# Attention kernel: shared units in another order, second layer norm on GpSimd, clamp checks in pairs

## What is computed

```python
def xattn(query, key_value, Wq, bq, Wk, bk, Wv, bv, Wo, bo):
    q, k, v = ...
    attn = jnp.einsum('bhqd,bhkd->bhqk', q, k) * scale
    attn = jnp.clip(attn, -CLAMP, CLAMP)
    attn = jax.nn.softmax(attn, axis=-1)
    x = jnp.einsum('bhqk,bhkd->bqhd', attn, v).reshape(B, Nq, Cq)
    return x @ Wo + bo
x = x + jnp.tanh(g_xattn[0]) * xattn(_layernorm(x, axis=-1), ctx_768, ...)
x = x + jnp.tanh(g_ffn[0]) * ffn(_layernorm(x, axis=-1), ...)
```

## Time and profile before

| | |
|---|---|
| median of 3 runs | 2075.0 us (2073.8 to 2075.75) |
| profiled execution | 2074.38 us, of which the span of instructions is 2072.6 us |
| TensorE / VectorE / ScalarE / GpSimd busy | 95% / 61% / 35% / 5% of the span |
| mean granted TensorE clock | 0.975 of full speed |
| attention stage | from about 105 us to 609 us |

### The profile page before, as it was taken

One profiled execution on the slowest core, in us unless ns is written; L12 is line 12 of the kernel. 1 busy time (PEld: TensorE's weight loads), 2 busy tenths in 40 slices (PEclk: granted clock), 3 DMA queues, 4 the chain that ended last, 5 costly groups with the idle time before them and its releaser, 6 DMA issues.

```text
span 2072.6 us, 29677 instructions
## 1 busy us (share of the span) xinstructions
PE 1978.3 (95%) x9252; PEld 1426.3 (69%) x9252; DVE 1271.3 (61%) x2415; ACT 725.1 (35%) x1206; POOL 102.0 (5%) x294
## 2 busy tenths in 40 slices
PE   7899999999958999999999999999999999999998
PEld 5734333333337877888888888888888888888887
DVE  5588888888626675555565465456456546555544
ACT  4447666666722222222222222222222222222222
POOL 4201001110111000000000000000000000000000
PEclk9979999999969999999999999999999999999999
DMA  7832222222110010000010010001010001000100
GB/s 242 328 105 78 78 79 69 80 69 69 38 42 21 0 64 32 31 10 15 26 35 16 31 30 15 10 26 40 11 31 31 15 10 48 18 10 10 46 30 36
DMA packets 76457, 102.47 MB, mean 49 GB/s; under 512 B 29026, under 2 KB 47204, under 8 KB 74340
## 3 DMA queue, kind: packets, MB, share of 16 engines
q1 hardware_dynamic: 76388, 101.67, 15.7%
HBM read 75.81 MB, written 25.56 MB: 49 GB/s over the span
## 4 chain that ended last, share of the span: by engine, by line
PE 69%; DVE 1%; ACT 0%; issue 0%; DVEq 0%; ACTq 0%
PE ps_h L1878 35%; PE ps_y L1892 35%; DVE h_lo L2099 0%; DVE h_hi L2095 0%; ACT gelu L1998 0%; DVE gated L2164 0%; ACT L1998 0%; DVE out_T_acc L2169 0%; DVE w_lo L2040 0%; DVE w_lo L2207 0%; DVE w_hi L2038 0%; PE ps_h L1960 0%; PE ps_h L1928 0%; DVEq L2233 0%; DVEq L2094 0%
## 5 line engine op out<-in xcount | busy, mean ns | idle before, releaser
L1998 ACT ACTIVATE gelu<-ps_h,b 128x512 f32<-128x512 f32 x512 | 352.7, 689 | 1084.1 <-PE ps_h L1878 1018.3
L2095 DVE CAST h_hi<-gelu 128x512 fp32r<-128x512 f32 x512 | 219.7, 429 | 575.6 <-ACT gelu L1998 570.1
L1878 PE MATMUL ps_h<-x_hi,w_hi 128*128 (+1 forms) x1024 | 409.2, 400 | 10.1 <-DVE w_lo L2040 8.8
L1892 PE MATMUL ps_y<-h_hi,w_hi 128*128 128x512 f32 x1024 | 405.1, 396 | 6.1 <-DVE h_lo L2099 6.1
L1878 PE MATMUL ps_h<-x_lo,w_hi 128*128 (+1 forms) x1024 | 406.0, 396 | 0.0
L1878 PE MATMUL ps_h<-x_hi,w_lo 128*128 (+1 forms) x1024 | 405.7, 396 | 0.0
L1892 PE MATMUL ps_y<-h_lo,w_hi 128*128 128x512 f32 x1024 | 404.9, 395 | 0.0
L1892 PE MATMUL ps_y<-h_hi,w_lo 128*128 128x512 f32 x1024 | 404.8, 395 | 0.0
L2099 DVE TENSOR_TENSOR h_lo<-gelu,h_hi 128x512 fp32r<-128x512 f32 x512 | 357.3, 698 | 16.5
L957 DVE TENSOR_REDUCE low<-ps_s 128x1 f32<-128x512 f32 x512 | 321.8, 682 | 41.2 <-PE ps_s L814 39.1
L1071 ACT ACTIVATE probs_T<-ps_t 128x512 f32<-128x512 f32 x384 | 207.5, 599 | 106.9 <-PE ps_t L824 104.8
(11 more groups left out here) (210 smaller groups left out, 1218.3 us busy)
## 6 DMA issues: line engine op xcount, KB each, us to landing
gate<-gates_scratch SPq DMA_DIRECT2D x64, 256.0 KB, 3.1
q_st<-q_scratch SPq DMA_DIRECT2D x192, 64.0 KB, 2.2
k_st<-k_scratch SPq DMA_DIRECT2D x192, 64.0 KB, 2.3
k_scratch<-k_hl SPq DMA_DIRECT2D x8, 1024.0 KB, 3.9
q_scratch<-q_hl SPq DMA_DIRECT2D x8, 1024.0 KB, 5.1
w_raw<-in_w1T SPq DMA_DIRECT2D x8, 1024.0 KB, 5.1
w_raw<-in_w2T SPq DMA_DIRECT2D x7, 1024.0 KB, 5.3
v_scratch<-v_out SPq DMA_DIRECT2D x8, 544.0 KB, 5.2
```

Of the source, the lines that this page charges most:

```text
L1878: mm = pe.matmul(ps_h[:, j % RING, :], w[:, k, at], x[:, k, bass.ds(c * SEQ, SEQ)], start=(i == 0), stop=(i == len(parts) - 1))
L1892: mm = pe.matmul(ps_y[s][:, d, :], w[:, j, at], h[:, j % RING, :], start=(j == 0 and i == 0), stop=(j == HT - 1 and i == 2))
L1998: act.activation(gelu[:, j % GELUS, :], ps_h[:, j % RING, :], ACT.Gelu_apprx_tanh, bias=b1[p][:, j:j + 1]).then_inc(gelu_done, 1)
L2095: dve.tensor_copy(h_hi[:, j % RING, :], gelu[:, j % GELUS, :]).then_inc(h_hi_done, 1)
```

## The change

1. The table `SHARED` is rewritten. `low` goes from the end places of (0, 0), (1, 0), (2, 0), (3, 0) to those of (0, 1), (1, 1), (2, 1), (3, 1). The two `out` units that stood at the ends of (1, 1) and (2, 1) go to the middles of (1, 2) and (2, 1). `rows`, the first `y` and `logits` move to the end places of (0, 2), (0, 3), (1, 0) and (3, 0). `x2T`, `xnT`, `pick` and the second `y` stay.
2. The scaling of the second norm goes from VectorE to GpSimd, directly behind the reciprocal root: one subtraction and one multiplication with broadcast operands for the first 128 tokens, and three instructions with both operations for the others.
3. `low` holds all four groups, and the checks cover two groups in one pair of instructions, at (0, 0) and (2, 0).

```diff
@@ -545,15 +545,17 @@
 SHARED = {
-    (0, 0, 1): ("low", 0, 1), (0, 1, 0): ("out", -1, 3), (0, 1, 1): ("rows", -1, 0),
-    (0, 2, 1): ("rows", -1, 1), (0, 3, 1): ("y", -1, 0), (1, 0, 1): ("low", 0, 2),
-    (1, 1, 0): ("y", -1, 1), (1, 1, 1): ("out", 0, 0), (1, 2, 1): ("x2T", -1, 0),
-    (1, 3, 1): ("x2T", -1, 1), (2, 0, 1): ("low", 0, 3), (2, 1, 1): ("out", 0, 1),
-    (2, 2, 1): ("xnT", -1, 0), (2, 3, 1): ("xnT", -1, 1), (3, 0, 1): ("low", 1, 0),
-    (3, 1, 0): ("out", 0, 2), (3, 1, 1): ("logits", -1, 0), (3, 3, 0): ("pick", -1, 0),
+    (0, 1, 0): ("out", -1, 3), (0, 1, 1): ("low", 0, 1), (0, 2, 1): ("rows", -1, 0),
+    (0, 3, 1): ("rows", -1, 1), (1, 0, 1): ("y", -1, 0), (1, 1, 0): ("y", -1, 1),
+    (1, 1, 1): ("low", 0, 2), (1, 2, 0): ("out", 0, 0), (1, 2, 1): ("x2T", -1, 0),
+    (1, 3, 1): ("x2T", -1, 1), (2, 1, 0): ("out", 0, 1), (2, 1, 1): ("low", 0, 3),
+    (2, 2, 1): ("xnT", -1, 0), (2, 3, 1): ("xnT", -1, 1), (3, 0, 1): ("logits", -1, 0),
+    (3, 1, 0): ("out", 0, 2), (3, 1, 1): ("low", 1, 0), (3, 3, 0): ("pick", -1, 0),
 }
-NORM_STEPS = {(1, 1): ("statistics", 0), (1, 2): ("statistics", 1), (2, 1): ("normalised", 0), (2, 2): ("normalised", 1)}
+STATISTICS = {(1, 1): 0, (1, 2): 1}
+CHECKS = {0: 0, 2: 1}
+MOMENTS = 10
 STEPS = [(g, k) for g in range(GROUPS) for k in range(TT)]
@@ -615,7 +617,7 @@
         bo_gated = n_.sb("bo_gated", [P, DIM])
-        low = n_.sb("low", [P, 2, GROUP * TT])
+        low = n_.sb("low", [P, GROUPS, GROUP * TT])
         low_rows = n_.sb("low_rows", [GROUP * TT, P], F32R)
@@ -625,7 +627,7 @@
         x_res = n_.sb("x_res", [P, TT, DIM])
-        fits = n_.sb("fits", [P, 3, GROUP * TT])
+        fits = n_.sb("fits", [P, 3, 2 * GROUP * TT])
         xn = n_.sb("xn_b", [P, TT, DIM])
@@ -765,7 +767,7 @@
                 mean, dev, diff, square, spread, var, root, root_2, scaled, rstd = (moments[:, i, :] for i in range(10))
-                first = b * 9
+                first = b * MOMENTS
                 pool.wait_ge(stats_done, b * 2 + 2)
@@ -794,12 +796,22 @@
+            def layer_norm(b):
+                pool.wait_ge(rstd_done, b + 1)
+                wait(pool, in_psum["xnT"], b * KT)
+                pool.tensor_tensor(xn[:, 0, :], x_res[:, 0, :], moments[:, 0, 0:1].to_broadcast([P, DIM]), ALU.subtract).then_inc(moment_done, 1)
+                for t in range(1, TT):
+                    pool.tensor_scalar(xn[:, t, :], x_res[:, t, :], moments[:, 0, t:t + 1], moments[:, 9, t:t + 1], ALU.subtract, ALU.mult)
+                pool.wait_ge(moment_done, b * MOMENTS + MOMENTS)
+                pool.tensor_tensor(xn[:, 0, :], xn[:, 0, :], moments[:, 9, 0:1].to_broadcast([P, DIM]), ALU.mult).then_inc(xn_ready, 2)
+
             with pool.Fori(0, BATCH) as b:
                 reciprocal_root(b)
+                layer_norm(b)
...
@@ -947,22 +959,22 @@
                 if t == 0 and u == 0:
-                    wait(dve, in_psum["low"], group_no(b, g) - 1)
-                    wait(dve, lows_checked, group_no(b, g) - 1)
+                    wait(dve, in_psum["low"], group_no(b, g) - GROUPS + 1)
+                    wait(dve, lows_checked, b * 2 + g // 2 - 1)
                 for i in (2 * u, 2 * u + 1):
                     column = (j % 2) * 2 * TT + (j // 2) * TT + t
-                    dve.tensor_reduce(low[:, g % 2, column:column + 1], ps_s[BANK_OF[at]][:], AX_X, ALU.min).then_inc(low_done, 1)
-
-            def check_lows(b, g):
-
-                dve.wait_ge(low_done, group_no(b, g) * GROUP * TT + GROUP * TT)
-                wait(dve, lows_checked, group_no(b, g))
-                dve.scalar_tensor_tensor(out=fits[:, 0, :], in0=low[:, g % 2, :], scalar=FITS, in1=fits[:, 0, :],
-                                         op0=ALU.is_le, op1=ALU.add)
-                dve.scalar_tensor_tensor(out=fits[:, 1, :], in0=low[:, g % 2, :], scalar=-FITS, in1=fits[:, 1, :],
+                    dve.tensor_reduce(low[:, g, column:column + 1], ps_s[BANK_OF[at]][:], AX_X, ALU.min).then_inc(low_done, 1)
+
+            def check_lows(b, pair):
+
+                dve.wait_ge(low_done, (group_no(b, 2 * pair + 1) + 1) * GROUP * TT)
+                wait(dve, lows_checked, b * 2 + pair)
+                lows = low[:, 2 * pair:2 * pair + 2, :].rearrange("p g n -> p (g n)")
+                dve.scalar_tensor_tensor(out=fits[:, 0, :], in0=lows, scalar=FITS, in1=fits[:, 0, :], op0=ALU.is_le, op1=ALU.add)
+                dve.scalar_tensor_tensor(out=fits[:, 1, :], in0=lows, scalar=-FITS, in1=fits[:, 1, :],
                                          op0=ALU.is_ge, op1=ALU.add).then_inc(lows_checked, 1)
...
@@ -998,15 +1010,6 @@
                 ins.then_inc(stats_done, 1)
-
-            def layer_norm(b, i):
-                if i == 0:
-                    dve.wait_ge(rstd_done, b + 1)
-                    wait(dve, in_psum["xnT"], b * KT)
-                for t in (2 * i, 2 * i + 1):
-                    ins = dve.tensor_scalar(xn[:, t, :], x_res[:, t, :], moments[:, 0, t:t + 1], moments[:, 9, t:t + 1],
-                                            ALU.subtract, ALU.mult)
-                ins.then_inc(xn_ready, 1)
@@ -1035,13 +1038,10 @@
                             take_unit(b, STEPS[STEPS.index((g, k)) - 1] + (1,))
-                        kind, i = NORM_STEPS.get((g, k), (None, 0))
-                        if kind and exists(b - 1):
-                            {"statistics": statistics, "normalised": layer_norm}[kind](b - 1, i)
-                        if k == 0:
-                            behind = group_after(b, g, 1)
-                            if exists(behind[0]) and exists(b):
-                                check_lows(*behind)
+                        if (g, k) in STATISTICS and exists(b - 1):
+                            statistics(b - 1, STATISTICS[g, k])
+                        if k == 0 and g in CHECKS and exists(b):
+                            check_lows(b, CHECKS[g])
                         take_unit(b, (g, k, 0))
...
```

More of the change, by code:

```diff
@@ L840, in turn_lows @@
                 pe.wait_ge(low_done, group_no(b, i) * GROUP * TT + GROUP * TT)
-                return pe.transpose(ps_m[0:GROUP * TT, 0:P], low[:, i % 2, :], ident[:])
+                return pe.transpose(ps_m[0:GROUP * TT, 0:P], low[:, i, :], ident[:])
             def turn_out(ps_m, b, i):
@@ L975, in normalise @@
                 dve.reciprocal(recip[:], heads[:, :, :, HDIM]).then_inc(recip_done, 1)
-                count = fits[:, 2, :].rearrange("p (t j) -> p t j", t=TT)
+                count = fits[:, 2, 0:GROUP * TT].rearrange("p (t j) -> p t j", t=TT)
                 dve.scalar_tensor_tensor(out=count, in0=heads[:, :, :, HDIM], scalar=SUM_LEAST, in1=count,
@@ L1052, in _ @@
                         lows(0, g, t, u)
-                if g == 0:
-                    check_lows(0, 0)
             batches(dve, batch)
-            dve.wait_ge(lows_checked, BATCH * GROUPS)
+            dve.wait_ge(lows_checked, BATCH * 2)
             dve.wait_ge(taken["out"], BATCH * GROUPS)
```

## The result

Median of the changed kernel: **2088.3 us** (2086.8 to 2089.6, 4 runs), against 2075.15 for the kernel before beside it; ratio 1.0064 [1.0047, 1.0082]. It is slower by 13.2 us where I had said 7.5, and within the range. The span of the profiled execution went from 2072.6 to 2087.7, by 15.1 us. I cut both spans where the first exponential of a batch starts (ScalarE's timeline), and behind batch 7 where the last exponential starts.

| part | forecast | measured | before: us, at 1.2 GHz | after: us, at 1.2 GHz |
|---|---|---|---|---|
| batch 0 | +0.5 | +2.6 | 48.9, 10.5 | 51.5, 15.5 |
| batches 1 to 6 | +4.55 | +0.7 | 348.7, 17.1 | 349.4, 3.4 |
| batch 7 | +0.95 | **+9.5** | 54.2, 0.9 | 63.6, 22.4 |
| behind it | +1.7 | +2.6 | 1494.7, 43.5 | 1497.3, 45.9 |

The account below looks back on a forecast made before the run. A loop batch was taken to be bound by TensorE and VectorE waiting for each other. Terms: 2074.4 + 0 + 5.7 - 0.2 + 1.7 + 0.5 = 2082.1, stated as 2082.5 us for the median; range 2063 to 2091.

Parts of the forecast that it names:

- batch 7: The last batch: forecast longer only by the sixth loop-entry delay of a check by GpSimd's addition, +0.95 us.
- (1, 1): Step of a steady batch: the second `y` waits until the first is added; 5.7 us, +0.4.
- (1, 2): Step of a steady batch: `x2T` waits for the taking of a middle `out`; 4.0 us, +0.3 together with (1, 3).
- (2, 2): Step of a steady batch: VectorE's `out` taking and half-norm scaling are gone, leaving TensorE's own 2.9 us; -1.15.
- (3, 0) with (3, 1): Steps where logits and minima change places and the middle `out` waits for a longer copy; 8.3 us, +0.35.
- The collision: Check at (0, 0) waits for GpSimd's later addition, delaying (0, 1)'s sums: +0.95 us at six entries, batches 2 to 7, +5.7.
- The ledger of the order: Step-by-step sum of the reordering in a steady batch: -0.1 to 0, called 0.0 us a batch.
- the entry into batch 1, -0.2: At the entry into batch 1, a check blocked before would no longer be blocked: -0.2 us.
- the scaling: GpSimd's five norm instructions at 613 ns each, 3.1 us (2.3 to 4.9); uncovered after the last batch, +1.7 (0.9 to 3.5).
- Rival 3: Clock also falls in the other three loop batches, just behind their start: 2089.5 us; chance 0.10 together with Rival 4.
- Rival 4: Check of (2, 0) waits for GpSimd's whole scaling: 1.2 us a batch more, 2090; chance 0.10 together with Rival 3.
- Rival 2: VectorE is the real bound, so work leaving it comes back: 2066 us, or 2059 with waits going too; chance 0.22.

Follow-up runs that it names:

- experiment 1: The changed kernel with its two paired checks one group later, at (1, 0) and (3, 0): 2081.3 us, 1.0043.
- experiment 2: The changed kernel with the old `SHARED` table; norm on GpSimd and paired checks stay: 2071.2 us, 0.9985.
- experiment 3: The kernel before with the new `SHARED` table alone; norm on VectorE, checks a group at a time: 2085.9 us, 1.0061.
- experiment 4: The changed kernel with the second norm's scaling back on VectorE at (2, 1) and (2, 2); new table and paired checks stay: 2085.8 us, 1.0063.
- experiment 7: The changed kernel with 32 extra plain scores, which nothing reads, in groups 2 and 3 of batch 7: 2080.1 us, 1.0026.
- experiment 8: The kernel before with 32 extra scores, which nothing reads, in batch 7: 2073.1 us, 0.9997.
- experiment 6: The changed kernel with the norm of the last batch alone scaled by VectorE again: 2079.7 us, 1.0029.
- experiment 5: The kernel before with the norm's scaling on GpSimd alone; old table, checks a group at a time: 2072.3 us, 0.9986.
- experiment 9: The changed kernel with both the last norm on VectorE and the 32 extra unread scores in batch 7: 2075.0 us, 1.0009.

## Why the prediction was right, and where not

**Right: the sign, the mechanism at the loop entries, and the steps.** Forecast and measured in us: (1, 1) 5.7 and 5.70; (1, 2) 4.0 and 3.96; (2, 2) 2.9 and 2.97; (3, 0) with (3, 1) 8.3 and 8.26; the whole batch at full clock 58.0 and 57.93. Experiment 1 shows that the collision is a cause and not a bystander; experiments 2 and 3 show that the order of units carries the loss. That the total came near is in part luck: the clock took some 5 us off the loop and put some 7 on batch 7, and the sum had neither.

**The steady batch was right by two errors that cancel.** "The collision" was +0.95, and measured 0.55. I took the check to be due 0.63 us into GpSimd's addition; it was due 0.93 in (296.55 - 295.62), since the addition moved by 4.25 us and not 4.55 against the batch's first exponential (from 3.71 ahead of it to 0.54 behind), so it was held 0.3 us less. The walk's own legs, 236.1 and 0.42, also give 0.9 and not 0.95. The sums now come 2.67 us behind the due check (299.22 - 296.55), where they came 2.05 behind it before (235.61 - 233.56): +0.62 by the walk, 0.55 by experiment 1. The ledger of the order, which I called 0.0, measured +0.3 (57.4 against 57.07). The terms add up to -0.12, so they are 0.4 short together, and no one of them is to blame: (2, 0) with (2, 1) gave +0.61 for +0.5, (2, 2) gave -1.06 for -1.15, (3, 0) with (3, 1) +0.39 for +0.35, (0, 2) to (1, 0) +0.08 and (3, 2) with (3, 3) +0.06 for 0, (1, 2) with (1, 3) the +0.3 forecast.

**Wrong: "the entry into batch 1, -0.2".** A check is held there too, 2.09 us instead of 0.97: the addition starts at 178.51 and the check at 178.84. I had counted that the old overlap would go, and had not worked out where the new one falls. It costs 1.4 us there (experiment 1).

**Wrong: batch 7, forecast at the collision's 0.95 alone.** This is the step that failed. I multiplied the steady batch and never walked the last one. In it VectorE has no minima in groups 2 and 3, so step (2, 2) was 2.65 us before, as the starts of (2, 2) and (2, 3) show:

```profile
558.01 0.66 PE L824 MATMUL ps_t<-q_st,k_st 49*128 49x512 f32 x2
560.66 0.66 PE L824 MATMUL ps_t<-q_st,k_st 49*128 49x512 f32 x2
```

The new table has no -1.15 to give there: in experiment 4 the step is 2.58, while the waits for an `out` in the middle remain. Experiments 4, 7 and 8 put the whole of it at 2.2 to 2.35 us, the collision included. On top came the clock: 22.4 us of batch 7 at 1.2 GHz, where it had been 0.9, worth the other 7.2. Why it fell there is open, below.

**Mis-sized: the scaling.** Three double operations of GpSimd at 1.22 us each are the upper end of my bound (twice 613 ns), not the 613 that I took. The five are 4.84 us instead of 3.1; the time behind batch 7 grew by 2.6, inside 0.9 to 3.5. The Trainium skill ("GPSIMD Engine Reference", "4.1 Engine selection") puts one-input elementwise work roughly at line rate on GpSimd. The row speaks against it: 1.22 us for what four of VectorE's did in 1.38 us together; a two-input one took half as long, 0.61.

**Rival 3 came half true, in another place.** The clock did not fall further at the loop entries. In the whole loop it stood lower for 3.4 us instead of 17.1. That is why five batches that are each 0.86 longer at full clock, and batch 1, which is 1.6 longer (58.73 in experiment 6), show only +0.7 together. It fell in batches 0 and 7 instead, by 5.0 and 21.5 us more. At the price that the earlier trace rows give, 2.5 us for a batch whose clock was 0.94 (some 7 us at the lower level), a microsecond of low clock costs 0.35, and 5.0 such make 1.8 of batch 0's +2.6. (Of the three loop batches that I called 0.94, one, 405.7 to 464.1, was 0.97, with 3.4 us of it.) From batch 0 to the experts the changed kernel had 15.2 us more of it, which is 5.3 us of the 15.1. The other 10 are the order, the collision and GpSimd's last norm: 0.8 in batch 0, some 5.5 in the loop, some 2 in batch 7, and some 1.8 behind, each as what is left of the part when its clock is taken off at that price.

**Rival 4** (the check of (2, 0) held by the whole scaling) did not happen: 0.18 us in six of the seven batches. **Rival 2** was wrong for this table and right for the old one: there a lighter VectorE does come back, 1.04 us a batch (experiment 2), nearly all at the very step, (2, 2), that it named. Under the new table 0.5 of it does (experiment 4).

**Open.** Why experiment 6 changes the clock of batches 0 and 7, which run the same instructions before its edit acts, isn't settled, nor why the clock fell in batch 7 of the changed kernel. That the kernels differ in it is no accident of one execution, since every run has its mean granted clock on record. The four runs of the changed kernel have 0.972 to 0.976, on average 111 us at the lower level (an estimate from clock and span); the 60 of the kernel before that stand beside the experiments have 0.974 to 0.979, on average 96. At 0.35 us each those 15 us more are again 5 of the 13 us of loss. Runs of one kernel differ by it too: those of experiment 5 went from 2063.9 us at clock 0.980 to 2076.9 at 0.971, which is 0.34 us of time for one at the lower level. So the split of the 15.1 us into 10 and 5 does not hang on the two executions profiled; where in the program the low clock fell is known from one profiled execution of each kernel.

## What to carry to other kernels

Price a hand-written order in each version of its body, above all the drained last one: an item that pays for itself in the steady loop has nothing to pay with where the other engine has less work. When a unit moves, follow its DMAs to the engine that waits for them, and look at what runs beside that. Where an engine is relieved, change only what relieves it: here the norm on GpSimd with the old order won 0.14%, and the reordering around it lost more than that.

## What the runs showed of the hardware that was not expected

- A check of VectorE (two operands in SBUF) was held in these traces only by GpSimd's instructions with two operand tensors. Beside three TENSOR_SCALARs of GpSimd from 267.89, which read `x_res` in SBUF too, it took 0.18 us at 268.54, with 0.5 us of the first of them left; it was so in six batches. In the seventh, at 557.59, it fell into the two-operand subtraction at 557.50, and took 0.57. The rule of the Trainium skill ("SBUF — State Buffer", "SBUF: two separate sides") asks only that GpSimd's instruction reads SBUF; here the measurement decides. Experiments 6, 7 and 9 show the same, each in six batches and the seventh. All 16 checks of the changed kernel, min, median and max in ns:

```profile
L976 DVE SCALAR_TENSOR_TENSOR fits<-low,fits x16: 178/375/2094, 127.5 to 557.6; 128x32 f32<-128x32 f32 x16
```

- More matmuls made a stretch shorter: 32 scores that nobody reads went with a granted clock of 1.00 instead of 0.82 in batch 7, and took 6.5 us off it (one profiled execution each; the whole time fell by 0.0038 of the kernel before, 7.9 us, in the median of eight runs). Where the clock had not been low (experiment 8) they cost 0.75.
